# ScalarE makes the turned one-hots and weighs a quarter of the rows; VectorE's products go over four tiles and two banks

## What is computed

```python
q, k, v = x @ Wq + bq, x @ Wk + bk, x @ Wv + bv        # heads of 32
s = (q[dst] * k[src]).sum(-1) / sqrt(32)               # one number per edge and head
w = exp(s - segment_max(s, dst)[dst])
out = segment_sum(w * v[src], dst) / segment_sum(w, dst)
```

## Time and profile before

| | |
|---|---|
| median of 3 runs | 7087.34 us (7085.92 to 7090.16) |
| the profiled execution | 7089.84 us, its span 7088.0 us |
| busy over the span | PE 4556.0, DVE 4541.5, POOL 4510.1, ACT 1771.3 us |
| turned one-hot on VectorE (L1409) | 0.75 us over 2048 elements, 1.27 over 4096 |
| mean granted clock of TensorE | 0.762 |
| edge passes (span of each, about) | L=0 to 1240; L=1 1510 to 3060; L=2 3230 to 4410; L=3 4560 to 5730; L=4 from 5900 |

### The profile page before, as it was taken

The page is one execution under the profiler, slowest core; times in us unless marked ns, Lnnn a source line. Parts: engine busy times, 40 slices in busy tenths (PEclk is TensorE's granted clock), DMA queues, the critical chain, the costliest instruction groups (busy, mean ns, idle before and its releaser), DMA issues.

```text
span 7088.0 us, 101780 instructions
## 1 busy us (share of the span) xinstructions
PE 4556.0 (64%) x17172; PEld 3057.5 (43%) x17173; DVE 4541.5 (64%) x12192; ACT 1771.3 (25%) x4933; POOL 4510.1 (64%) x4940
## 2 busy tenths in 40 slices
PE   3555555867777777785666766566666635555556
PEld 1433343444444444463444444344444423433343
DVE  5555554558998998874666666655656564544446
ACT  0000000523333333343333433433333340000004
POOL 5777776145555555516777776277777737777771
PEclk6777777977887888886777777777777767777776
DMA  3333334378888888845444445244444453333334
GB/s 81 105 105 105 105 105 100 108 240 291 291 293 288 291 292 291 284 135 148 129 129 129 128 129 108 78 135 129 129 134 129 126 132 105 105 105 105 105 104 89
DMA packets 499049, 1084.13 MB, mean 153 GB/s; under 512 B 105385, under 2 KB 296492, under 8 KB 491469
## 3 DMA queue, kind: packets, MB, share of 16 engines
q0 software_dynamic: 240064, 696.46, 35.4%
q1 hardware_dynamic: 258603, 384.24, 16.2%
HBM read 1010.63 MB, written 71.05 MB: 153 GB/s over the span
## 4 chain that ended last, share of the span: by engine, by line
PE 30%; POOL 22%; issue 20%; DVE 17%; DVEq 5%; DMA 3%; ACT 2%; POOLq 0%; ACTq 0%; SPq 0%
POOL ring L685 21%; PE bank L929 17%; DVE acc L1367 5%; PE bank L974 2%; DVE aux L1429 2%; DVE ring L1509 2%; PE bank L1156 2%; PE bank L987 2%; DMA ring<-g_t,stage 2%; DVE ohc L1373 1%; PE bank L1109 1%; DVE sc L1419 1%; DMA aux<-q_t 1%; DVEq L1367 1%; DVEq L1612 1%
## 5 line engine op out<-in xcount | busy, mean ns | idle before, releaser
L929 PE MATMUL bank<-ring,ohc 128*128 128x256 f32 (+3 forms) x8800 | 3080.4, 507 | 1372.5 <-DMA ring<-xs_t,stage 399.1
L929 PEld LDWEIGHTS bank<-ring,ohc 128*128 128x128 f32 x8800 | 2069.7, 250 | 2223.5 <-issue 1056.6
L1367 DVE TENSOR_TENSOR acc<-acc,bank 128x256 f32 (+3 forms) x4400 | 1857.0, 422 | 1475.3 <-PE bank L929 1325.8
L685 POOL DMA_INDIRECT ring<-g_t,stage x1760 | 1769.1, 1005 | 521.7 <-issue 480.6
L685 POOL DMA_INDIRECT ring<-kv_t,stage x880 | 863.6, 981 | 667.4 <-PE bank L929 422.0
L685 POOL DMA_INDIRECT ring<-in_x,stage x880 | 834.5, 948 | 273.8 <-issue 256.4
L685 POOL DMA_INDIRECT ring<-xs_t,stage x880 | 834.1, 948 | 260.8 <-issue 256.9
L744 ACT ACTIVATE ohc<-iota,rel_c 128x128 f32<-128x128 f32 x1760 | 558.1, 388 | 243.5 <-PE bank L929 243.2
L793 ACT ACTIVATE aux<-bank 128x512 f32<-128x512 f32 (+1 forms) x26 | 14.9, 572 | 2227.6 <-PE bank L1098 2227.6
L1509 DVE TENSOR_TENSOR ring<-ring 128x1024 f32<-128x1024 f32 (+1 forms) x550 | 554.9, 1009 | 9.4
L765 ACT ACTIVATE cl<-cl 128x1 f32<-128x1 f32 (+3 forms) x111 | 22.5, 203 | 2151.7 <-DVE mx L1502 2151.7
(11 more groups left out here) (274 smaller groups left out, 3914.9 us busy)
## 6 DMA issues: line engine op xcount, KB each, us to landing
aux<-q_t SPq DMA_DIRECT2D x880, 192.0 KB, 5.0
aux<-relb_t SPq DMA_DIRECT2D x56, 1024.0 KB
relx<-relb_t SPq DMA_DIRECT2D x55, 512.0 KB
ring<-g_t,stage POOLq DMA_INDIRECT x1760, 2.8
x<-ring SPq DMA_DIRECT2D x21, 896.0 KB, 4.3
ring<-x SPq DMA_DIRECT2D x21, 896.0 KB, 9.4
mk<-mk SPq DMA_DIRECT2D x445, 32.1 KB
ring<-in_x,stage POOLq DMA_INDIRECT x880, 2.8
```

Source lines behind the costliest of these rows:

```text
L685: g_.indirect_dma_start(out=rings[L][:, slot, 0:W], out_offset=None, in_=table[L][:, :], in_offset=bass.IndirectOffsetOnAxis(ap=stage[:, s ...
L929: return mm(agp[k % 4][:, 0:width], ohc[:, hot, :], rg[:, slot, vo:vo + width], start=True, stop=True)
L1367: tt(win, win, agp[k % 4][:, 0:width], ALU.add).then_inc(p["added"], 1)
```

## The change

- `hot_turned` moves from VectorE to ScalarE in all three softmax passes, as 1 - |difference| cut off at zero in two activations; in ScalarE's round it comes after the fourth `hot_four` (8-head) or amid the eight (4-head), and in the 1-head pass first.
- In the 8-head pass ScalarE weighs the last four tiles of batch c, 32 activations of 32 elements, each with its own scale, between the third and the fourth `hot_four`; TensorE waits for them on a semaphore `wa` at tile 12. VectorE weighs three times instead of four.
- `dest_rows`, `products` and `reduce` cover four tiles each. `qe4` are two pairs of PSUM banks; window sums get three banks instead of four in this pass, and the chain's `m0` and `m1` share the fourth. `prod` has one buffer where it had two half as large.
- The orders of VectorE and TensorE in the 8-head round are written anew, and SP issues query rows in fours.

The diff, cut to its core:

```diff
-        agp, qe, m0, m1 = banks[0:4], banks[4:6], banks[6], banks[7]
+        agp, qe = banks[0:4], banks[4:6]
+        qe4 = [psum[:, 2048:3072], psum[:, 3072:4096]]
+        AGP = [4, 3, 4, 4, 4]
+        M0 = [None, banks[3], banks[6], banks[6], None]
+        M1 = [None, banks[3], banks[7], banks[7], None]
-        prod = aux[:, 3072:4096].rearrange("p (r t w) -> p r t w", r=2, t=2)
+        prod = aux[:, 3072:4096].rearrange("p (t w) -> p t w", t=4)
...
-                                if k % 2 == 0:
-                                    wait(sp, p["qe"], b * 8 + (k // 2 - 1))
+                                if k % 4 == 0:
+                                    sp.wait_ge(p["qe"], b * 4 + (k // 4 + 1))
...
+                    def hot_turned(b, par):
+
+                        act.wait_ge(p["rx"], b * 16 + (16 * past(L) + 16))
+                        act.activation(turned[L][par], relb[L], ACT.Abs, scale=-1.0, bias=iota_p[:, 0:1])
+                        act.drain()
+                        act.activation(turned[L][par], turned[L][par], ACT.Relu, scale=-1.0, bias=onesm[:, 0:1])\
+                            .then_inc(p["oht"], 1)
...
+                        for g in range(min(hots, 3)):
+                            hot_four(c, g)
+                        if L == 1 and sums:
+                            for k in range(12, 16):
+                                for h in range(H):
+                                    part = rg[:, cset * G + k, 256 + 32 * h:288 + 32 * h]
+                                    ins = act.activation(part, part, ACT.Copy, scale=rg[:, cset * G + k, po_ + h:po_ + h + 1])
+                            ins.then_inc(p["wa"], 1)
+                        for g in range(3, min(hots, 4)):
+                            hot_four(c, g)
+                        if feed:
+                            hot_turned(b + 1, (o + 1) % 2)
+                        for g in range(4, hots):
+                            hot_four(c, g)
...
-                            pe.wait_ge(p["added"], b * G + (k + 1 + summed(L)))
+                            free = 4 if L == 1 and k == 0 else 5 - AB
+                            pe.wait_ge(p["added"], b * G + (k + free + summed(L)))
...
-                        pe.wait_ge(p["prod"], b * 8 + r + 1)
-                        pe.wait_ge(p[f"qw{r % 4}"], b * 64 + 32 * (r // 4) + 32)
-                        for j in range(2):
-                            k = 2 * r + j
+                        pe.wait_ge(p["prod"], b * 4 + r + 1)
+                        for j in range(4):
+                            k = 4 * r + j
+                            if j % 2 == 0:
+                                pe.wait_ge(p[f"qw{k // 2 % 4}"], b * 64 + 32 * (k // 8) + 32)
...
-                            for g in range(3):
-                                if scores:
-                                    dest_rows(b, par, 2 * g + 2)
-                                    dest_rows(b, par, 2 * g + 3)
-                                sums_of(4 * g, 4 * g + 4)
+                            if scores:
+                                dest_rows(b, par, 2)
+                            sums_of(0, 4)
+                            if scores:
+                                dest_rows(b, par, 3)
+                            sums_of(4, 12)
...
-                            pair(1)
-                            dots(1)
                             if sums:
                                 begin_sums(c, window_at(cp, 0), cp)
                             weigh_four(0)
                             if scores:
                                 load_offsets(b, par, 0)
                             weigh_four(1)
+                            pair(1)
+                            add(0, 2)
+                            dots(1)
+                            add(2, 4)
+                            weigh_four(2)
                             pair(2)
-                            add(0, 1)
+                            add(4, 6)
                             dots(2)
...
                             dots(3)
...
-                            if feed:
-                                hot_turned(b + 1, (o + 1) % 2)
+                            add(10, 12)
                             if scores:
                                 ch1(b, par, ub)
```

More of the change, by code:

```diff
@@ L86, in fours, with weighed @@
     return sum(TS[1:L]) // 4
+def weighed(L):
+    return (0, 0, 3 * NB, 3 * NB + TS[2] // 4)[L]
 def staged(L):
@@ L213, in gnn_kernel @@
         lnst = sb("lnst", [128, 16, 12])
-        banks = [ctx.enter_context(nc.psum_tensor(f"bank{k}", [128, 512], F32)) for k in range(8)]
-        agp, qe, m0, m1 = banks[0:4], banks[4:6], banks[6], banks[7]
+        psum = ctx.enter_context(nc.psum_tensor("bank", [128, 8 * 512], F32))
+        banks = [psum[:, 512 * k:512 * k + 512] for k in range(8)]
+        agp, qe = banks[0:4], banks[4:6]
[3 more added lines that the diff above has]
+        M1 = [None, banks[3], banks[7], banks[7], None]
+        HEAD = [None, 128, 0, 0, None]
+        TAIL = [None, 256, 128, 128, None]
+        ONES = [None, 400, 272, 272, None]
         upper = lambda v_: v_.bitcast(BF16)[..., 1::2]
@@ L748, in hot_four @@
                                        bias=onesm[:, 0:1]).then_inc(p["oc"], 1)
+                    def hot_turned(b, par):
[4 more added lines that the diff above has]
+                            .then_inc(p["oht"], 1)
+                    hot_turned(0, 0)
                     def chain(i, o, scores, sums):
                         b, rset, _, par, _ = batch_at(L, i, o)
-                        c, _, _, _, _ = batch_at(L, i, o - 1)
-                        if sums and L < 3:
-                            for g in range(tiles_of(L, c) // 4):
-                                hot_four(c, g)
+                        c, cset, _, _, _ = batch_at(L, i, o - 1)
+                        feed = scores and (not isinstance(b, int) or b + 1 < NBS[L])
+                        hots = tiles_of(L, c) // 4 if sums and L < 3 else 0
+                        for g in range(min(hots, 3)):
[12 more added lines that the diff above has]
+                            hot_four(c, g)
                         if not scores:
@@ L911, in _ @@
                 rg = rings[L]
-                vo, width = VALS[L], SUMS[L]
+                vo, width, AB = VALS[L], SUMS[L], AGP[L]
+                m0, m1, head, tail, ones_at = M0[L], M1[L], HEAD[L], TAIL[L], ONES[L]
                 q = NODE[L]
@@ L927, in window_sum @@
                 def window_sum(slot, hot, k):
-                    return mm(agp[k % 4][:, 0:width], ohc[:, hot, :], rg[:, slot, vo:vo + width], start=True, stop=True)
+                    return mm(agp[k % AB][:, 0:width], ohc[:, hot, :], rg[:, slot, vo:vo + width], start=True, stop=True)
                 if not H:
@@ L1035, in cols_of @@
                             gate(pe, p["ch2"], b + (past(L) + 1))
-                            mm(m1[0:R, 264:265], rows[0:1, 3, 0:R], ones[0:1, 0:1], start=True, stop=True)
-                            mm(m1[0:R, 265:266], rows[0:1, 4, 0:R], ones[0:1, 0:1], start=True, stop=True).then_inc(p["col"], 1)
+                            mm(m1[0:R, ones_at - 8:ones_at - 7], rows[0:1, 3, 0:R], ones[0:1, 0:1], start=True, stop=True)
+                            mm(m1[0:R, ones_at - 7:ones_at - 6], rows[0:1, 4, 0:R], ones[0:1, 0:1], start=True, stop=True).then_inc(p["col"], 1)
                         def turn_back():
@@ L1537, in batch @@
                         c, cset, _, cp, _ = batch_at(L, i, o - 1)
-                        feed = scores and (not isinstance(b, int) or b + 1 < NBS[L])
                         def add(k0, k1):
```

88 lines of the change are left out of this document (32 added, 56 removed).

## The result

The changed kernel took 7199.05 us (median of 4 runs, 7195.12 to 7210.88) beside 7086.63 of the kernel before (7084.14 to 7090.16): a ratio of 1.0161, 95% interval 1.0143 to 1.0179. The prediction had 7114 with 7015 to 7180: the side was right, the time was 85 us too low and outside the range.

A forecast was written before the change was run, and what follows sets the result against it. VectorE was taken to bound the 8-head pass, POOL the 4-head and 1-head passes. +58 us for 54 batches, +5 tail and -39 late passes gave +24 on 7089.84, so 7114 us; range 7015 to 7180.

The forecast's parts named there:

- VectorE's savings: VectorE, 8-head pass: fewer weighs, no turned one-hot, larger products and sums save 2.41 us, 25.54 a batch if nothing waits.
- ScalarE, cost nothing: ScalarE, 8-head pass: its added weighs (6.9 us) and one-hot (4.1) delay nothing, with 0.6 us to spare.
- plus 0.3: 8-head batch: first two window adds 0.5 us apart and last sums drained in full add 0.3 us.
- The clock: TensorE, 8-head pass: lower clock level at the turn, higher one after it; a batch 29.03 us, +1.08.
- E: Time mark in the 8-head pass: the end of a batch's last chain operation on VectorE (L1502).
- (e): TensorE at batch end: 24 matmuls instead of 12 before the weights' turn back, which comes at E+4.0, or E+1.25.
- (f): SP's query rows of tiles 8 to 11 wait for 12 matmuls; VectorE's first window add stalls 3.6 us, or 2.1.
- w: Time mark in the 8-head pass: end of the weights' turn back, put at E+5.2, or E+2.45 when fast.
- no stall at all: Bound for the 8-head pass: VectorE never waits at the first window add, -2.41 us a batch or -130.
- Late passes: 4-head and 1-head passes: without VectorE's turned one-hot, POOL's gathers shorten, -19.4 us in each pass, -39 together.
- The faster one: 8-head pass: small stall, first window add before about E+8; 7034 us, without a stall 6926; chance 0.30.
- The slower one: TensorE, 8-head pass: the clock falls in the new gap too, +134 us there, 7190 in all; chance 0.13.

The follow-up runs named there:

- e8: Changed kernel with the turned one-hots made by VectorE again: 7277.95 us, ratio 1.0269 to the kernel before.
- e11: Changed kernel with the first four window sums ahead of the product matmuls of tiles 8 to 11 on TensorE: 7029.34 us, ratio 0.9908 to the kernel before.
- e10: Kernel before with the first twelve window adds of an 8-head batch two by two instead of one by one: 7170.54 us beside 7094.01, ratio 1.0108.
- e17: Changed kernel with window sums ahead of late query rows, first ten adds one by one and reductions halved: 6980.91 us, ratio 0.9831 to the kernel before.
- e12: Changed kernel with the first ten window adds one by one and each reduction in two halves: 7114.29 us, ratio 1.0031 to the kernel before.

## Why the prediction was wrong

**VectorE's savings, 2.41 a batch.** The one-hot's 0.67 is borne out (e8: 38.9 us in the pass, predicted 36). The fourth weigh's 1.14 was not tested alone. Four-tile products and sums have the predicted distance: in e11 from the product at 2224.05 to the add at 2225.19 it is the 1.14 taken, from the sum at 2226.09 to the add at 2227.22 the 1.13. Neighbours that need not wait again start closer than their lengths (this product is 1.22 long, this sum 1.21). The larger distance appears where one has to wait for the other, in the pairs of adds: 0.90 for a pair in e10, where two single adds take 0.66.

**ScalarE, cost nothing.** Right. 32 weighs take 6.88 us (predicted 6.9), a turned one-hot 1.99 and 2.00 (4.1). It waits 468.6 us for the chain in the pass. Only its busy time was added up wrong: "some 650 us more" leaves out the late passes' one-hots, and it became 990, of which the one-hots are 618 (e8).

**The step that failed** is the last term of the batch: "plus 0.3 (the first two adds 0.5 apart, the last sums drained in full) = 29.03". The new order on VectorE, add(0, 2), add(2, 4) and so on, stood in the diff, and I costed every add but the first two at the 0.33 of the earlier trace rows, where each stands between other instructions. A pair takes 0.24 more than that. e10 measures 76.5 us for six pairs alone, and between e11 and e17 five of them, less the halved reductions, are 48. The row that would have told stood in VectorE's timeline of the kernel before, where adds 14 and 15 of every batch come side by side, and was not read:

```profile
2214.80 1.00 DVE L1367 TENSOR_TENSOR acc<-acc,bank 128x264 f32 x2
```

Two adds of 0.43 end 1.00 after the first start, so the second begins 0.57 behind the first.

**The clock, the second step that failed.** "I take the lower level at the turn, where single-column matmuls of the chain are as now, and the higher one after it." The lower level, a granted clock of 0.50, holds at the score turn in 22 of 51 batches, and the higher one does not last: in all 51 the clock falls between E and the first window add, in 40 of them while TensorE stands idle for query rows, and in 49 the granted clock from the last query rows' matmuls to that add is below 0.6 (mean 0.51). That stretch takes 2.56 us in the mean (predicted 1.5), and the second add comes 0.93 behind the first (0.5).

**(e) and (f), the stall.** The cause was right; that its end was right within 0.3 us in the mean (E+10.54, predicted 10.2) is luck in part. The sum took the slow batch's 24 matmuls for every batch (5.30 us in the batch shown, 3.96 in the mean), so the last rows' matmuls start 0.7 earlier than predicted, and the lower clock takes 1.06 back. One part of the working was wrong: I had VectorE ready at E+6.6, but its correction waits for w, which the prediction itself had at E+5.2. So even in e11, where the rows no longer hold it up, the first add comes at E+7.46 in the mean, and the bound "no stall at all" was out of reach. TensorE waits for query rows 4.6 us a batch in the pass (251.1 us), a little above the 2 to 4 that were to show it.

Together, in a mean batch of 30.60 where 29.03 was predicted: the five pairs behind the first 1.15, the first two adds 0.43, the first add late by 0.34, the rest 0.35 less than the sum had. The pairs of e10 (76.5) and e12's gain (85) both come close to the miss of 85, and that is chance: neither is the whole of it, and what was late at one place was made good in part at another.

**Tail**, +5: from the last score turn to the first gather of the 4-head pass 157.6, where it was 155.2: +2.4. To this comes that the last two batches are 5.6 longer than the loop's +2.6 each gives. **Late passes**, -39: -38.7.

**The rivals.** The faster one decides at a first add before about E+8, and it comes at E+10.54. The slower one, a clock that falls in the new gap too, had its condition right, against the forecast's choice, and with 7190 comes nearest to 7199. But that is not the whole cause: the pairs are not in it, and the two alone would give 7266 without the early rows and the shorter chain. The 0.05 given to larger fixed costs was the author's estimate: no run shows such a cost, and the four-tile instructions of e11 start at the distances that the prediction took (1.14 and 1.13).

## To carry to other kernels

What an add costs here depended on its neighbour, 0.33 us behind an instruction that it need not wait for and 0.57 behind the add that it waits for: before pricing an edit that reorders, look whether two instructions of which one waits for the other come side by side, and take the row of such a pair. In TensorE's program, work whose input had long been there belonged ahead of work whose input was still on its way: three moved lines were worth 170 us (e11). When one part of a change is tried alone, look first at the loop's branch: this one part cost 171 us alone and gained 73 beside the rest. Before a term is taken from one batch, look how many others are like it: the price of the 24 matmuls was that of the slowest kind, 5.30 us where the mean was 3.96.

## What was not expected of the hardware

- A VectorE add of 264 elements that waits by semaphore for the add just ahead of it starts 0.57 us behind that one; another instruction that need not wait starts 0.33 behind it. Twelve adds in six pairs cost 76.5 us of 7094 with no instruction more.
- In the changed kernel TensorE's granted clock fell from 1.00 to 0.50 between E and the first window add in each of 51 batches, in 40 of them while TensorE stood idle for query rows; in e11, where window sums fill that time, the next score turn was at 0.50 once in 51, in the changed kernel 22 times.
- VectorE stood still for 8 us at a loop's branch in every round (209.5 us in 25) while the instruction queue moved packets, in a kernel with fewer instructions than the one without that cost.
- The kernel before takes 7087 or some 8400 us, at a mean granted clock of 0.76 to 0.77 or 0.70 to 0.71, and one chip can be in either condition; and the ratio of two kernels is another in each.
